# First batch of a four-stage residual kernel: an activation table loaded at the front, x added by TensorE, a bias split moved to GpSimd, and VectorE's order by halves

## The reference, cut to what matters

```python
def _L0_cond_ref(hidden_states, language_ids, W1, b1, W2, b2, gamma, beta):
    w1 = W1[language_ids]                      # 256 x 64 for each batch
    w2 = W2[language_ids]                      # 64 x 256
    h = jnp.einsum('bsh,bha->bsa', hidden_states, w1) + b1[language_ids][:, None, :]
    h = jax.nn.relu(h)
    adapted = jnp.einsum('bsa,bah->bsh', h, w2) + b2[language_ids][:, None, :]
    x = hidden_states + adapted
    mean = jnp.mean(x, axis=-1, keepdims=True)
    var = jnp.mean(jnp.square(x - mean), axis=-1, keepdims=True)
    normed = (x - mean) * jax.lax.rsqrt(var + LN_EPS)
    return normed * gamma[language_ids][:, None, :] + beta[language_ids][:, None, :]

x = x + _L0_cond_ref(...)        # adapter and layer norm
x = x + _L1_cond_ref(...)        # x @ W[subject].T + b[subject], 256 x 256
x = x + _L2_cond_ref(...)        # two expert and three shared networks 256 -> 1024 -> 256, with gates
x = x + _L3_cond_ref(...)        # masked softmax pooling over the rows
```

## Time and profile before

| | |
|---|---|
| median of 3 runs | 525.22 us (524.85 to 525.82) |
| profiled execution, its own time | 524.68 us |
| span from first to last instruction | 522.9 us |
| mean granted TensorE clock | 0.993 |
| PE busy | 509.9 us (98%) |
| DVE busy | 329.5 us (63%) |
| ACT busy | 266.1 us (51%) |
| POOL busy | 238.5 us (46%) |
| transfers | 49.31 MB, mean 94 GB/s |

### The profile page before, as it was taken

One profiled execution on the slowest core, in us unless ns is written; L12 is line 12 of the kernel. 1 busy time (PEld: TensorE's weight loads), 2 busy tenths in 40 slices (PEclk: granted clock), 3 DMA queues, 4 the chain that ended last, 5 costly groups with the idle time before them and its releaser, 6 DMA issues.

```text
span 522.9 us, 7047 instructions
## 1 busy us (share of the span) xinstructions
PE 509.9 (98%) x2463; PEld 422.9 (81%) x2465; DVE 329.5 (63%) x606; ACT 266.1 (51%) x508; POOL 238.5 (46%) x205
## 2 busy tenths in 40 slices
PE   8899999999999999999999999999999999999986
PEld 5688888888888788888888788888888878888974
DVE  7688224884676674786467675687367676435386
ACT  4565554443557563545266564445355647444253
POOL 2655455445344443443535433434544434734034
PEclk9999999999999999999999999999999999999997
DMA  5624442222224323323143422322222223420002
GB/s 172 202 107 132 104 137 102 81 81 81 81 81 131 102 80 88 132 66 113 52 137 97 145 89 81 121 81 80 81 81 81 80 81 104 139 81 1 1 0 81
DMA packets 44539, 49.31 MB, mean 94 GB/s; under 512 B 7380, under 2 KB 34264, under 8 KB 44504
## 3 DMA queue, kind: packets, MB, share of 16 engines
q1 hardware_dynamic: 42888, 47.03, 28.0%
q10 hardware_dynamic: 1616, 1.84, 1.0%
HBM read 46.76 MB, written 2.10 MB: 93 GB/s over the span
## 4 chain that ended last, share of the span: by engine, by line
PE 91%; DVE 5%; ACT 2%; ACTq 1%; POOL 1%; issue 1%; DVEq 0%
PE ps_hid L801 14%; PE ps_hid L806 13%; PE ps_hid L802 13%; PE ps_net L858 13%; PE ps_net L859 13%; PE ps_net L863 13%; PE ps_net L830 2%; PE ps_side L554 1%; PE ps_side L662 1%; PE ps_side L478 1%; PE ps_side L482 1%; PE ps_side L477 1%; DVE att_split L1386 1%; PE ps_side L488 1%; PE ps_side L491 1%; PE ps_side L530 1%
## 5 line engine op out<-in xcount | busy, mean ns | idle before, releaser
L1705 DVE SCALAR_TENSOR_TENSOR hid_lo<-ps_hid,hid_hi 128x512 fp32r<-128x512 f32 x160 | 110.4, 690 | 165.8 <-ACT hid_hi L1068 164.8
L1801 POOL TENSOR_TENSOR wi_lo<-raw_wi,wi_hi 128x512 fp32r<-128x512 f32 x78 | 104.1, 1334 | 225.3 <-ACT wo_hi L1049 121.2
L1068 ACT ACTIVATE hid_hi<-ps_hid 128x512 fp32r<-128x512 f32 x160 | 95.4, 597 | 208.9 <-PE ps_hid L806 208.2
L801 PE MATMUL ps_hid<-x2T_hi,wi_lo 128*128 128x512 f32 (+1 forms) x332 | 125.9, 381 | 0.3 <-POOL wi_lo L1799 0.3
L802 PE MATMUL ps_hid<-x2T_hi,wi_hi 128*128 128x512 f32 (+1 forms) x332 | 125.3, 380 | 0.0
L858 PE MATMUL ps_net<-hid_hi,wo_hi 128*128 128x512 f32 x304 | 120.8, 397 | 0.0
L859 PE MATMUL ps_net<-hid_hi,wo_lo 128*128 128x512 f32 x304 | 118.8, 391 | 0.0
L1802 POOL TENSOR_TENSOR wo_lo<-raw_wo,wo_hi 128x512 fp32r<-128x512 f32 x78 | 101.5, 1301 | 0.0
L806 PE MATMUL ps_hid<-x2T_lo,wi_hi 128*128 128x512 f32 (+1 forms) x332 | 99.1, 380 | 0.0
L863 PE MATMUL ps_net<-hid_lo,wo_hi 128*128 128x512 f32 x304 | 93.9, 390 | 0.0
L801 PEld LDWEIGHTS ps_hid<-x2T_hi,wi_lo 128*128 128x128 f32 x332 | 62.4, 188 | 12.4 <-POOL wi_lo L1799 0.5
(11 more groups left out here) (324 smaller groups left out, 532.2 us busy)
## 6 DMA issues: line engine op xcount, KB each, us to landing
raw_wi<-in_L_cond_share_wi_dram SPq DMA_DIRECT2D x23, 512.0 KB, 3.7
raw_wo<-in_L_cond_share_wo_dram SPq DMA_DIRECT2D x23, 512.0 KB, 4.8
raw_wi<-in_L_cond_expert_wi_dram SPq DMA_DIRECT2D x16, 512.0 KB, 3.7
raw_wo<-in_L_cond_expert_wo_dram SPq DMA_DIRECT2D x16, 512.0 KB, 4.7
x_rows<-in_x_dram SPq DMA_DIRECT2D x3, 512.0 KB, 5.9
out_dram<-out_rows SPq DMA_DIRECT2D x6, 256.0 KB, 5.1
gate_w<-in_L_cond_gate_w_dram SPq DMA_DIRECT2D x1, 1024.0 KB, 5.5
subj_w<-in_L_cond_weight_dram SPq DMA_DIRECT2D x3, 256.0 KB, 2.7
```

What stands on the lines that cost most here:

```text
L801: mm(dst, wi_lo[:, w, k, c], x2T_hi[:, k, rows], start=(k == 0), stop=False)
L1068: fn(hid_hi[:, ring(b, q)], ps_hid[:, ring(b, q)], ACT.Relu).then_inc(hid_hi_ready, 1)
L1705: v.scalar_tensor_tensor(out=hid_lo[:, ring(b, q)], in0=ps_hid[:, ring(b, q)], scalar=0.0, in1=f32(hid_hi[:, ring(b, q)]), op0=ALU.max, op ...
L1801: g.tensor_tensor(wi_lo[:, w], raw_wi[:, half % 2, :, c], f32(wi_hi[:, w]), ALU.subtract)
```

## The change

Only batch 0's prologue is changed, and the order in which two parameters are loaded in all batches.

- ScalarE runs a copy of one element behind the issues of x, so that its table load stands there and no longer ahead of `opT_hi`.
- w2 is loaded ahead of b1.
- b2 is split by GpSimd behind `w2_lo`, no longer by VectorE. The upper copy of `w2_hi` is made by VectorE from w2, no longer by ScalarE.
- The adapter's product has one bank to a row tile (`adapted_bank`: two in `ps_net`, two in `ps_hid`). TensorE multiplies the identity with `x_rows` into it in float32 first. VectorE's addition is gone, and statistics and normalisation read PSUM.
- TensorE transposes `subj_w` between the two halves of the adapter. Fillers: 2, 2, 5, 5 become 0, 0, 3, 7.
- VectorE makes `subj_wT_lo` between the statistics of half 0 and its normalisation, and `x1_lo(0)` ahead of `add_norm(1)`. ScalarE makes `xbT` of half 1 behind the normalisation of half 0, and the high part of `wo` of pair 1 ahead of `x1_hi(1)`.

```diff
-    WARM_XT, WARM_ADAPT, WARM_SUBJ, WARM_NORM, WARM_HALF, WARM_OUT = 7, 2, 2, 5, 5, 6
+    WARM_XT, WARM_NORM, WARM_HALF, WARM_OUT = 7, 3, 7, 6
...
+        def adapted_bank(r):
+
+            return (ps_net[:, 0], ps_net[:, 1], ps_hid[:, 0], ps_hid[:, 1])[r][:, 0:D]
+
...
                     sp.dma_start(w1[:], L0_W1[la].rearrange("o (k p) a -> p (o k) a", p=P)).then_inc(w1_in, 16)
+                    sp.dma_start(w2[:], L0_W2[la].rearrange("o a d -> (o a) d")).then_inc(w2_in, 16)
                     sp.dma_start(b1[:], L0_b1[la].rearrange("o a -> a o")).then_inc(b1_in, 16)
-                    sp.dma_start(w2[:], L0_W2[la].rearrange("o a d -> (o a) d")).then_inc(w2_in, 16)
...
+            def adapted_rows(h):
+
+                tiles = [(adapted_bank(r), r) for r in (2 * h, 2 * h + 1)]
+                for dst, r in tiles:
+                    mm(dst, ident[:], x_rows[:, r], start=True, stop=False)
+                pe.wait_ge(p_pool.sem, p_pool.at(0, "w2_hi"))
+                pe.wait_ge(p_dve.sem, p_dve.at(0, f"hlo{h}"))
+                pe.wait_ge(p_act.sem, p_act.at(0, f"hup{h}"))
+                for dst, r in tiles:
+                    mm(dst, hT_both[:, r * P:(r + 1) * P], w2_hi[:], start=False, stop=False)
+                pe.wait_ge(p_pool.sem, p_pool.at(0, "b2_lo"))
+                for dst, r in tiles:
+                    last = mm(dst, hT_hi[:, r * P:(r + 1) * P], w2_lo[:], start=False, stop=True)
                 return last
...
-                keep_warm(WARM_ADAPT, warm)
-                for h in range(2):
-                    pe.wait_ge(p_pool.sem, p_pool.at(0, "w2_lo"))
-                    pe.wait_ge(p_dve.sem, p_dve.at(0, f"hlo{h}"))
-                    pe.wait_ge(p_act.sem, p_act.at(0, f"hup{h}"))
-                    adapt_half(ps_net[:, h], h).then_inc(p_pe.sem, 1)
-                keep_warm(WARM_SUBJ, warm)
+                adapted_rows(0).then_inc(p_pe.sem, 1)
                 pe.wait_ge(subj_in, 16)
                 transpose_subj(ps_net[:, 2], True).then_inc(p_pe.sem, 1)
+                adapted_rows(1).then_inc(p_pe.sem, 1)
                 keep_warm(WARM_NORM, warm)
...
+            act.wait_ge(zeros_ready, 2)
+            fn(score_col[:, 0:1], ones[:, 0:1], ACT.Copy)
             subj = act.value_load(subj_id.rearrange("(o b) -> o b", o=1)[0:1, 0:1], min_val=0, max_val=L1_weight.shape[0] - 1)
...
-            act.wait_ge(p_pool.sem, p_pool.at(0, "w2_hi"))
-            fn(w2_hi[A:P], f32(w2_hi[0:A]), ACT.Copy).then_inc(p_act.sem, 1)
...
-                fn(norm[:, r], norm[:, r], ACT.Identity, bias=neg_shift[:, r:r + 1], scale=rstd[:, r:r + 1]).then_inc(p_act.sem, 1)
+                fn(norm[:, r], adapted_bank(r), ACT.Identity, bias=neg_shift[:, r:r + 1], scale=rstd[:, r:r + 1]).then_inc(p_act.sem, 1)
...
+            x_beta(0)
+            act.wait_ge(p_pe.sem, p_pe.at(0, "subj_wT"))
+            fn(subj_wT_hi[:].rearrange("p k d -> p (k d)"), ps_net[:, 2], ACT.Copy).then_inc(p_act.sem, 1)
             normalise(0)
+            x_beta(1)
             split_weights(0, 0, False)
             normalise(1)
             x1_hi(0)
             fn(wi_hi[:, 1], raw_wi[:, 0, :, 2 * P:4 * P], ACT.Copy)
+            fn(wo_hi[:, 1], raw_wo[:, 0, 2:4], ACT.Copy).then_inc(w_hi_ready, 1)
             x1_hi(1)
-            fn(wo_hi[:, 1], raw_wo[:, 0, 2:4], ACT.Copy).then_inc(w_hi_ready, 1)
...
-                def add_x(h):
+                def statistics(h):
                     dve.wait_ge(p_pe.sem, p_pe.at(0, f"adapt{h}"))
-                    t = slice(2 * h, 2 * h + 2)
-                    done(v.tensor_tensor(norm[:, t].rearrange("p r d -> p (r d)"), ps_net[:, h], x_rows[:, t].rearrange("p r d -> p (r d)"), ALU.add))
-                    here(f"sum{h}")
-
-                def statistics(h):
+                    for j in range(2):
+                        last = v.bn_stats(stats[:, 2 * h + j], adapted_bank(2 * h + j))
+                    done(last)
+
+                def variance(h):
...
-                dve.wait_ge(b2_in, 16)
-                set_bias_row(v, dve, here, done)
+                dve.wait_ge(w2_in, 16)
+                done(v.tensor_copy(w2_hi[A:P], w2[:]))
...
-                add_x(0)
                 statistics(0)
-                add_x(1)
+                variance(0)
+                dve.wait_ge(p_act.sem, p_act.at(0, "subj_w_hi"))
+                done(v.tensor_tensor(subj_wT_lo[:].rearrange("p k d -> p (k d)"), ps_net[:, 2],
+                                     f32(subj_wT_hi[:].rearrange("p k d -> p (k d)")), ALU.subtract))
                 normalise(0)
                 statistics(1)
+                variance(1)
                 dve.wait_ge(gamma_in, 16)
                 add_norm(0)
                 normalise(1)
-                dve.wait_ge(p_act.sem, p_act.at(0, "subj_w_hi"))
-                done(v.tensor_tensor(subj_wT_lo[:].rearrange("p k d -> p (k d)"), ps_net[:, 2],
-                                     f32(subj_wT_hi[:].rearrange("p k d -> p (k d)")), ALU.subtract))
+                x1_lo(0)
                 add_norm(1)
-                x1_lo(0)
                 x1_lo(1)
...
+            pool.wait_ge(b2_in, 16)
+            set_bias_row(g, pool, lambda name: pool.wait_ge(p_pool.sem, p_pool.at(0, name)), lambda ins: ins.then_inc(p_pool.sem, 1))
```

More of the change, by code:

```diff
@@ L253, in cond_resid_program @@
         a_pool = Steps(sem("a_pool"), "w1_lo w2_lo rstd", 1)
[L255 to L259, removed]
+        p_pe = Steps(sem("p_pe"), "xT0 xT1 hid0 hid1 adapt0 subj_wT adapt1 normT0 normT1 y0 y1")
+        p_act = Steps(sem("p_act"), "xhi0 xhi1 hid0 hid1 hup0 hup1 xb0 subj_w_hi norm0 xb1 norm1 x1hi0 x1hi1")
+        p_dve = Steps(sem("p_dve"), "w1_hi xlo0 xlo1 w2_up hhi0 hlo0 hhi1 hlo1 stats0 aggr0 var_eps0 subj_w_lo norm0 "
+                                    "stats1 aggr1 var_eps1 x1T0 norm1 x1lo0 x1T1 x1lo1")
+        p_pool = Steps(sem("p_pool"), "w1_lo w2_hi w2_lo b2_hi b2_lo rstd0 shift0 rstd1 shift1")
         gate_sum = Steps(sem("gate_added"), "g0k0 g0k1 g1k0 g1k1 g2k0 g2k1 g3k0 g3k1")
@@ L518, in adapt_half @@
                 return last
+            def adapted_rows(h):
[10 more added lines that the diff above has]
+                    last = mm(dst, hT_hi[:, r * P:(r + 1) * P], w2_lo[:], start=False, stop=True)
+                return last
             def stage_a(slot, i, after_c):
@@ L1117, in _, with x_beta @@
             act.wait_ge(beta_in, 16)
-            for h in range(2):
+            def x_beta(h):
                 for k in range(KD):
@@ L1121, in _ @@
                 last.then_inc(p_act.sem, 1)
-            act.wait_ge(p_pe.sem, p_pe.at(0, "subj_wT"))
-            fn(subj_wT_hi[:].rearrange("p k d -> p (k d)"), ps_net[:, 2], ACT.Copy).then_inc(p_act.sem, 1)
             def normalise(h):
@@ L1594, in halves @@
                     return bank.rearrange("p (k s) -> p k s", k=KD)
-                def add_x(h):
+                def statistics(h):
                     dve.wait_ge(p_pe.sem, p_pe.at(0, f"adapt{h}"))
-                    t = slice(2 * h, 2 * h + 2)
-                    done(v.tensor_tensor(norm[:, t].rearrange("p r d -> p (r d)"), ps_net[:, h], x_rows[:, t].rearrange("p r d -> p (r d)"), ALU.add))
-                    here(f"sum{h}")
-                def statistics(h):
+                    for j in range(2):
+                        last = v.bn_stats(stats[:, 2 * h + j], adapted_bank(2 * h + j))
+                    done(last)
+                def variance(h):
                     rows = slice(2 * h, 2 * h + 2)
-                    for r in (2 * h, 2 * h + 1):
-                        last = v.bn_stats(stats[:, r], norm[:, r])
-                    done(last)
                     here(f"stats{h}")
@@ L1617, in normalise @@
                     dve.wait_ge(p_pool.sem, p_pool.at(0, f"rstd{h}"))
-                    done(v.tensor_scalar(norm[:, r], norm[:, r], aggr[:, r, 0:1], rstd[:, r:r + 1], ALU.subtract, ALU.mult))
+                    done(v.tensor_scalar(norm[:, r], adapted_bank(r), aggr[:, r, 0:1], rstd[:, r:r + 1], ALU.subtract, ALU.mult))
                 def add_norm(h):
@@ L1729, in _ @@
             v.memset(zeros[:], 0.0).then_inc(zeros_ready, 1)
-            v.memset(ones[:], 1.0)
+            v.memset(ones[:], 1.0).then_inc(zeros_ready, 1)
             v.memset(f32(edge_st[:]), 0.0)
```

## The result

The changed kernel takes 523.56 us (median of 7 runs, 523.41 to 524.73), the kernel before 525.4 beside it (7 runs, 524.85 to 526.03). The ratio is 0.9969, 95% interval 0.9958 to 0.9980: 1.6 us, or 0.31%, faster, between 0.2 and 0.42%. The two medians are 1.84 apart.

The account below looks back on a forecast made before the run. The prologue's chain of waits, ahead of a full TensorE, was taken to bound the kernel. The pair at 23.61 moves to 22.7, 0.9 us off the 525.22 median, giving 524.3; range 523.3 to 526.0.

Parts of the forecast that it names:

- What bounds it: The first 22 us are a chain; a shift of half 1's first x2T_lo pair, at 23.61, shifts the end.
- Likeliest case, A: Prologue chain with VectorE still waiting for GpSimd's splits: gain 0.9 us, from 0.5 to 1.3, time 524.3; chance 0.45.
- until 8.7: GpSimd's splits of w2 and b2, some 2.4 us from about 6.3 or b2's landing near 7.4, last until 8.7.
- The term on w2's earlier load: Prologue loads: w2 lands earlier, issued 0.7 us earlier, so GpSimd's split can start from about 6.3.
- b1: Prologue loads: b1 is issued one DMA (0.5 us) later, 4.2 against 3.68, and lands at 6.8, in time.
- the table load: ScalarE in the prologue: with the load at about 1.7, its first copy of xT0 starts at 5.25, 0.45 us earlier.
- The f32 products of x: TensorE ahead of the adapter: two products a half, 0.43 us each, 0.86 a half; half 0's lie in hlo0's wait.
- Rival B: VectorE's prologue: GpSimd holds nothing up, x1_lo(1) 0.9 to 1.1 us earlier; gain 1.7, time 523.5; chance 0.30.
- Rival C: VectorE's x1_lo(0) misses the gap, GpSimd's wo_lo goes first, y1 at 22.0; time 525.5, 0.3 above before; chance 0.14.
- Rival D: TensorE's clock at the lower level from 9.5 us on, after idling without fillers: 2.0 us slower, 527.2; chance 0.08.
- Rival E: The prologue's gain is real but absorbed later, say by GpSimd's pair 1: time 525.2; chance 0.03.

Follow-up runs that it names:

- e_b1_first: The changed kernel with the load of b1 issued ahead of that of w2 again, as before the change: 524.14 us.
- the repeat: The changed kernel once more, nothing altered: 523.80 us, 1.23 us below the kernel before by the medians and 1.6 by the ratio.
- e_x_dve: The changed kernel with x added by VectorE again and TensorE's float32 products of x left out: 525.32 us, ratio 0.9999 to the kernel before.
- e_order: The changed kernel with x1_lo(0) behind x1T of half 1, as before the change: 523.47 us.
- e_pair1_late: The changed kernel with GpSimd's split of pair 1 waiting for x1_lo(1): 523.11 us, 0.7 below the changed kernel in the same batch.

## Why the prediction was right, and where its sizes were off

**What bounds it** held. The prologue's chain sets the start of the row products, and a shift of the pair is a shift of the end: 1.26 at the pair, 1.16 at hid_lo of the last slots.

**Likeliest case, A,** held in its mechanism, step by step, in the profile of the changed kernel. The table load at 1.71; opT_hi at 5.24 (forecast 5.25); hT_hi held beside GpSimd's b2 rows, ending at 8.53 (8.9); hlo1 at 9.75 (10.1); statistics at 9.88 and 12.49 (10.15, 12.8); x1_lo(0) ending at 16.69 (17.1) with wo_lo 1.82 long (1.85); x1_lo(1) 1.46 long (1.4), ending at 19.64 (20.0); the pair at 22.35 (22.7). Everything is 0.3 to 0.4 early, and all of it enters at one term: "until 8.7" for GpSimd's b2. It ended at 8.38, because w2 was there by 5.90, not 6.3, and b2 by 7.18, not 7.4. The term on w2's earlier load was half a clause in the forecast, and is the 0.3 to 0.5 us of e_b1_first. Gain in the trace 1.26 for 0.9; measured 1.6 by the ratio in both batches, 1.84 and 1.23 by the medians. The 0.35 is within what one execution differs from the next: in the repeat's profile w2 was read at 6.55, and the statistics (10.13, 12.74) and the pair (22.58) stand nearly where the forecast had them. One term was late rather than early, b1, which was to be there at 6.8, in time:

```profile
7.18 1.09 ACT L1127 ACTIVATE hT<-ps_hid,b 64x256 f32<-64x256 f32 x2 [0.83 <-DMA b<-in_L_cond_b_dram]
```

TensorE's hidden product ended at 7.08, so hT lost at most 0.1 to it, which hT_hi, held by GpSimd in any case, did not feel.

**The time itself** lay outside A. A's own range was 523.9 to 524.7, and the forecast gave a gain of over 0.2% less weight (0.42) than no clear change (0.49). That 523.56 is inside the stated range is owed to the room made for B, and to that extent it is luck.

**How the gain was divided** was wrong in one place, and only the experiments show it. The forecast credited the table load with 0.45 at the start of opT_hi; taken back, it costs 0.13 us and the pair doesn't move. The addition alone is worth 0.7 to 0.8, w2 ahead of b1 another 0.3 to 0.6 once the addition is gone, and the bias, the table load and the order of the halves, undone one at a time, 0.13 us or less, which these times can't tell from nothing. The new order even needs the addition's move (e_x_dve).

**The f32 products of x:** 1.02 us in the profile for four instructions, starts 0.21 apart, in the time in which TensorE would have waited for hlo0: the 0.86 of starts that the forecast took.

**Rival B** (no waits, 523.5) has the measured time, but not the mechanism: hT_hi 0.77 and x1_lo(1) 1.46 show both waits. Half of B does happen in some executions: in the profiles of e_order and e_pair1_late, the same code up to there, hT_hi took its bare 0.28. The second wait is in all six profiles that have the changed kernel's order there and no hold on GpSimd's splits (x1_lo(1) 1.45 or 1.46). What it costs is e_pair1_late: counted from the statistics, x1_lo(1) ends 0.78 earlier without it, where B had 0.9 to 1.1, the pair 0.5, and the median is 0.7 lower.

**Rival C** did not happen, though the starts were as near as the forecast feared: 16.00 for opT_lo and 16.03 for wo_lo; in the repeat 16.25 and 16.28. Here VectorE's reported start is first, and by the rule of the Trainium skill (SBUF — State Buffer, the section on the two separate sides: whoever starts first holds the port pair) it would go first as well, so this pair does not separate the two readings. The trace agrees with the rule so far as it shows: wo_lo takes 1.82, its 1.28 and 0.54 more.

**Rival D** did not happen. TensorE idles 0.5 us ahead of the adapter (8.62 to 9.12), and behind it the products of 256 columns start 0.12 apart: the 2.4 GHz level, while the granted clock says 1.00.

**Rival E** did not happen: 9.99 of 10 us busy at 22 to 32.

## What to carry to other kernels

When a diff has many parts, price each one as if it stood alone, and then ask which of them meet at the same wait: here the early table load and the bias split end at the same hT_hi, and only the one that comes last counts. A short load at the head of a queue (w2 ahead of b1) can be worth nearly as much as a re-planned engine (0.3 to 0.6 us here, for 0.7 to 0.8), since it decides which operations of GpSimd and VectorE lie side by side. And before judging a shift by a span, find out what the tail does with it: a drop of the clock at the end can hide 1 us in one execution and not in the next.
